# Cross-attention and routed experts on one core: the transfers of x one turn earlier, and the expert's weight address read behind the up products

## The reference, cut to what matters

```python
x = x + xattn(layernorm(x), ctx)          # 16 heads of 16, keys and values from ctx
h = layernorm(x)
probs = softmax(h @ gate_w.T)             # 8 experts
topw, sel = top_k(probs, 2); topw /= sum(topw)
g, u = split(h @ w1[e].T)                 # 176 each
out  = (silu(g) * u) @ w2[e].T            # weighted by topw, summed over the two experts
x = x + out
```

## Time and profile before

| | |
|---|---|
| median of 3 runs | 459.46 us (458.37 to 460.66) |
| profiled execution, its own time | 459.9 us |
| its span, first to last instruction | 458.2 us |
| TensorE busy | 428.8 us, 94% |
| VectorE busy | 365.5 us, 80% |
| ScalarE busy | 298.1 us, 65% |
| GpSimd busy | 278.9 us, 61% |
| share of TensorE's lines in the chain that ended last | 86% |

### The profile page before, as it was taken

One profiled execution on the slowest core, in us unless ns is written; L12 is line 12 of the kernel. 1 busy time (PEld: TensorE's weight loads), 2 busy tenths in 40 slices (PEclk: granted clock), 3 DMA queues, 4 the chain that ended last, 5 costly groups with the idle time before them and its releaser, 6 DMA issues.

```text
span 458.2 us, 15236 instructions
## 1 busy us (share of the span) xinstructions
PE 428.8 (94%) x4422; PEld 381.7 (83%) x4422; DVE 365.5 (80%) x1283; ACT 298.1 (65%) x873; POOL 278.9 (61%) x472
## 2 busy tenths in 40 slices
PE   7899899999999999999999988799999999999980
PEld 3668788988889888898898877499999999898970
DVE  7558689898898988989999786669766666888993
ACT  4465767777677777777777754456666666666650
POOL 5773447687676767767777665664445444444451
PEclk9999999999999999999999999979999999999995
DMA  7234333544423433334343333554444445789965
GB/s 215 81 110 117 105 92 109 145 143 140 143 80 98 120 93 106 98 93 122 93 119 87 97 86 109 150 173 144 136 137 130 128 142 178 228 254 333 310 215 180
DMA packets 55818, 64.62 MB, mean 141 GB/s; under 512 B 9775, under 2 KB 49210, under 8 KB 55738
## 3 DMA queue, kind: packets, MB, share of 16 engines
q1 hardware_dynamic: 45034, 42.73, 33.1%
q0 software_dynamic: 6480, 16.85, 10.5%
q10 hardware_dynamic: 4224, 4.06, 2.7%
HBM read 32.73 MB, written 23.14 MB: 122 GB/s over the span
## 4 chain that ended last, share of the span: by engine, by line
PE 86%; DVE 4%; issue 3%; DMA 3%; ACT 2%; POOL 1%; SPq 1%; POOLq 0%; DVEq 0%; ACTq 0%
PE bank L1450 14%; PE bank L1452 13%; PE bank L1451 13%; PE bank L1513 6%; PE bank L1703 4%; PE bank L1501 4%; PE bank L1460 3%; PE bank L1574 3%; PE bank L1570 3%; PE bank L1571 3%; PE bank L1572 3%; PE bank L1478 3%; PE bank L1485 2%; PE bank L1556 2%; PE bank L1737 2%
## 5 line engine op out<-in xcount | busy, mean ns | idle before, releaser
L635 POOL DMA_INDIRECT expert_out<-probs,late x71 | 70.0, 986 | 73.7 <-ACT probs L836 71.5
L558 POOL DMA_INDIRECT sorted_rows<-row,place_i x64 | 68.4, 1068 | 34.7 <-POOL row L550 24.5
L1450 PE MATMUL bank<-we_h,xt_h 128*128 x142 | 52.6, 370 | 0.6 <-DVE xt_l L1363 0.6
L728 ACT ACTIVATE probs<-bank 128x1024 f32<-128x1024 f32 x32 | 32.9, 1027 | 23.3 <-PE bank L1574 23.3
L1451 PE MATMUL bank<-we_l,xt_h 128*128 x142 | 46.4, 326 | 0.0
L1452 PE MATMUL bank<-we_h,xt_l 128*128 x142 | 46.3, 326 | 0.0
L1373 DVE SCALAR_TENSOR_TENSOR probs<-xn,late,bank 128x176 f32<-128x176 f32 x71 | 28.0, 395 | 19.9 <-ACT xn L816 19.1
L816 ACT ACTIVATE xn<-bank 128x176 f32<-128x176 f32 x71 | 22.6, 318 | 31.2 <-PE bank L1452 31.2
L1363 DVE TENSOR_TENSOR xt_l<-bank,xt_h 128x256 fp32r<-128x256 f32 x71 | 30.1, 424 | 14.2 <-ACT xt_h L810 13.3
L972 DVE TENSOR_REDUCE bank<-bank 128x16 f32<-128x1024 f32 x32 | 39.1, 1222 | 0.0
L1574 PE MATMUL bank<-neg_max_t,head_of 128*128 128x128 bf16 x256 | 35.2, 219 | 0.0
(11 more groups left out here) (233 smaller groups left out, 1563.3 us busy)
## 6 DMA issues: line engine op xcount, KB each, us to landing
late<-sorted_rows SPq DMA_DIRECT2D x71, 129.0 KB, 2.3
we_f<-w_exp SPq DMA_DIRECT2D x32, 152.0 KB, 2.3
v_bd<-v_sb SPq DMA_DIRECT2D x128, 34.0 KB, 2.3
ctx_in<-ctx_t SPq DMA_DIRECT2D x32, 128.0 KB, 2.3
qp<-q_hl SPq DMA_DIRECT2D x128, 32.0 KB
x<-x SPq DMA_DIRECT2D x13, 256.0 KB, 2.9
row<-expert_out SPq DMA_DIRECT2D x6, 512.0 KB, 4.9
qp<-expert_out SPq DMA_DIRECT2D x6, 512.0 KB, 5.3
```

The source lines that it names most:

```text
L558: pool.indirect_dma_start(sorted_rows, bass.IndirectOffsetOnAxis(ap=place_i[:, t.slot // 2, k, t.par:t.par + 1], axis=0), row[:, k, t.slot ...
L635: pool.indirect_dma_start(expert_out, bass.IndirectOffsetOnAxis(ap=hs(r)[:, D:D + 1].bitcast(U32), axis=0), y_sb[:, r % YRING, :], None, b ...
L1450: pe.matmul(dst, a_h, b_h, start=start, stop=False)
```

## The change

The transfers of `x` begin in turn 0 and end in turn 11, where they began in turn 1 and ended in turn 12. The read of the next slot's weight address moves from ahead of the transposes of slot `i` to behind the up products of slot `i-1`; what is read there in turn `i` is the address of slot `i`, which the next turn uses. The address of slot 0 is read at the start of turn 0.

```diff
@@ SyncE, the turn of the first part
-            if 1 <= j * SKEW + s <= X_THIRD + X_REST:
-                n = j * SKEW + s - 1
+            if j * SKEW + s < X_THIRD + X_REST:
+                n = j * SKEW + s
                 at = 8 + 2 * n
                 sp.dma_start(x1[:, at:at + 2, :], x_v[:, at:at + 2, :]).then_inc(x_third if n < X_THIRD else x_rest, 16)
@@ TensorE, the turn of the second part
-            if gates:
-                found[r] = weights_of(i - 1)
+            if i == 0:
+                found[1] = weights_of(0)
             if i == 1:
                 pe.wait_ge(S["x_gate_ready"], NT)
                 pe.wait_ge(S["qn_ready"], NT)
             if not static or i < NSLOT:
                 tr_hs(i, r % 2, j, r)
             if i == 1:
                 warm(kv_bank, 3)
             if gates:
                 gate_up(i - 1, (r - 1) % 2, found[r])
+            if 1 <= i < NSLOT:
+                found[(r + 1) % RING] = weights_of(i)
```

## The result

| | before | change |
|---|---|---|
| median | 459.48 us, 4 runs (458.37 to 460.66) | 454.04 us, 4 runs (453.15 to 456.11) |
| profiled execution, its own time | 459.9 us | 456.11 us |
| its span | 458.2 us | 454.4 us |

The ratio is 0.9888, with an interval of 0.9845 to 0.9930: 5.4 us less, against 6.0 forecast. The profiled execution of the change is the slowest of its four. Part of that is its start: the first transpose of x stands at 10.7 us, before at 8.9.

A forecast was written before the change was run, and what follows sets the result against it. TensorE, busy 94% of the span, was taken as the bound, so only its idle or slowed places could win time. Gains of 3.1 + 2.5 + 0.5 = 6.1 us from 459.9 gave 453.8, forecast as 453.5 us; range 451.0 to 457.2.

The forecast's parts named there:

- The transfers of x: First part, turns 5 and 13: issued one turn earlier, both VectorE waits go, 3.1 us saved; bounds 2.0 and 3.2.
- The new transfer in turn 0: Start of the first part: issued at about 10.2 us behind the setup, delays nobody; cost taken as 0, at most 0.6.
- Rival C: First part: the earlier transfers win nothing because another wait replaces the one removed; 456.5 us, chance 0.05.
- The calm stretch: Second part, slots 6 to 48: a few hundredths saved in some turns, 0.5 us taken from 0 to 2.
- The reserve of 0.35 to 0.5: Second part: sequencer's lead over the array at the moved address read, 0.35 to 0.5 us instead of 0.17.
- Rival B: Second part: the activation's transposes starve behind the moved read, 0.2 us by 67 slots; about 470 us, chance 0.06.
- The late reads: Second part, slots 48 to 70: moved address loads cover overruns better, 2.5 us saved; bounds 0 and 4.5.
- about 2.08: Second part, from slot 48 on: forecast pace in us a slot, where before had 2.204.
- Rival A: Second part: the moved read wins nothing because the sequencer is nearly full, 1.8 of 2.0 us; 456.4 us, chance 0.17.
- The start of the second part: First turns of the second part: ScalarE and VectorE set the turn, so the moved reads cost 0.
- rival D: Start of the second part: TensorE's low clock lasts over more busy turns, up to 3 us given back; 456.5, chance 0.06.

The follow-up runs named there:

- the kernel with the earlier store: The change, with ScalarE's store of results issued about 1 us earlier, behind the activation function of the same turn: 457.36 us against 460.78, ratio 0.9951.
- the thin sums: The kernel before, with VectorE's sums of finished results (lines 1413 and 1418) on 4 of 256 columns: 456.46 us in one execution, before 460.39.
- the thin stores: The kernel before, with ScalarE storing finished rows of only 16 of 128 partitions: 454.82 us in one execution, before 460.78.
- rounds 1 and 2: Variants of the change there: sums and stores one turn later, 453.68 us; sums two turns later, 453.87; read behind the activation's transposes, 455.3.
- round 3: Before with stores of 16 partitions, 454.82 us, or later stores, 459.7; the change with earlier stores, 457.36, or a second unused read, 479.5.

## Why the prediction was right, and where not

**The transfers of x (3.1 us): right.** No wait of line 947 is left, the turns take 8.3 and 8.0 us where 8.1 was forecast, 1.8 + 1.1 = 2.9. The experiment with the transfers alone gives 3.7 us in the median, somewhat more, and no run shows why. Not all of the 2.9 arrives: the first transposes of the second part come 2.0 us earlier. Over all profiles that stretch takes 278.1 to 279.1 us with the early transfers, and 282.4 once (with the second read); without them it takes 280.7 to 281.1, and 282.7 and 285.8 once each. The new transfer in turn 0 costs nothing that shows. Rival C falls.

**The calm stretch (0.5): right.** 42 by 0.009 is 0.4 us.

**The reserve of 0.35 to 0.5: right in an ordinary turn, not for long loads.** The ordinary turn shows 0.4 to 0.5, but the long loads of the kernel with the earlier store were covered by 0.2 at the median. Rival B, the activation's transposes that starve, did not happen: the list has no wait of theirs for issue in the change from 388 to 440, and behind three of its four longest loads there (0.53 to 0.65) they came 0.1 to 0.2 us late.

**The late reads (2.5 us): the step that failed.** I wrote that "the six shrink by 0.3 each, 1.8 us, and the small ones go, 0.9", with loads as long as before. Four things were otherwise. The 0.3 for each load was too large: the new place covers some 0.2 of a long load where the old one covered 0.17, so with loads as long as before (excess 6.3) the waits for issue are 2.5 us in the new place and were 2.6 in the old. The loads themselves lost 4.3 to 5.5 us of excess, which no term held, because the new place begins with ScalarE's store and not 0.9 us behind it; shown by moving the store alone, which brought the long loads back. With the long loads the issue waits went altogether, so the pace should have come near 2.02, and with one turn more for the results it did. But the fourth thing took it back: VectorE now reaches the sum before the result has landed, and the slot waits behind it, 1.7 us in one profile; in the other 2.2 and some 1.75 by the clock that falls after it. What was left of the late stretch is 1.2 us in the one and 0.1 in the other profile, against 2.5, and its pace 2.15 and 2.20, where about 2.08 was named as the sign. I had bounded the term by how long loads are and how far they are covered, and had not asked the prediction's own question there, what is late next. The row that answers it was in reach, in the trace of before: the first ten transfers of results land 3.9 to 6.3 us after their issue there, while the sums are placed by a count of turns. The one issued at 410.6 landed 4.6 us later, and its sum began at 415.89, only 0.7 us behind. (The results come back from slot 45 on, the first is issued at 385.3, and not from about slot 51 as said above.)

**Rival A, that the read wins nothing,** is not excluded by the medians: the read is worth about 1 us, less than half of 3.0, and the interval of the read alone reaches none. Its reason is. The sequencer's count of 1.8 us was near the 1.7 found, but it did not bind; the results' transfer did.

**The sum.** 3.1 + 2.5 + 0.5 was forecast as the gain. In the medians it is 3.7 for the transfers and 1.3 for the read, 5.0, or 5.4 by the first comparison. That the total is so near is luck in part: the first part gave more than its term, and in the second a cover put too large and a wait put at nothing met loads that became shorter for a reason nobody had forecast. The start of the second part was costed at 0. The table shows 1.35 us less there in the change, but this goes with the clock: the lower level lasts 6.8 us before and in the transfers alone (6.9), where that stretch takes 16.4 us, 3.4 us in the change and in most others (15.0 to 15.6), and is absent in the thin sums (14.1). Kernels with the order of before stand in all three groups. So it varies with the execution. No loss of the kind of rival D shows at that place.

**Open** is why a register load grows behind a store. With fewer bytes, of loads or of stores, the loads were shorter, in one execution each. It is not the store's own bytes that a load meets, at least not always. The load of 1.31 us in before was over at 403.86, and from 402.5 to 403.9 the view of the DMA queues has only these two:

```profile
q1 hardware_dynamic: 75, 0.31, 70.9%
q0 software_dynamic: 1, 0.00, 0.7%
```

The stores are in queue 10 (its bytes fall from 4.06 to 0.62 MB with the thin stores), so the store issued at 401.65 had not moved a byte yet. The load of 1.18 us with the earlier store is the same case: no packet of queue 10 from 393.2 to 394.5. What such a load does meet no row tells, nor why a distance of 1.9 to 2.6 us can be long again. Open too is whether the later sums are worth having: they save 4.0 us up to slot 70 and give back 1.6 behind it in one pair of profiles, and the medians do not decide.

## What to carry to other kernels

When a wait shrinks in a pipeline that is paced by one engine, look at everything that is placed by a count of turns and waits for a transfer: faster turns bring its consumer forward, not its data. Give it the turn that was won, and check what that adds behind the last turn. And an instruction whose duration varies with traffic is placed by its distance from the transfers that are issued near it, not only by what covers it.

## What the runs showed of the hardware

- A register load on TensorE's sequencer takes 0.30 us as a rule. While results are stored and loaded back it took over 0.4 and up to 1.55 in 45 of the 50 cases in which it began about 0.9 us behind the issue of a whole 256 KB store, and at most 0.32 in the 59 cases of the change and its variants of rounds 1 and 2 in which it began within 0.25 us of it, before or behind. In round 3 two of 16 that began within 0.3 us of the issue, before or behind it, were long (0.57 and 0.83), so the place is a good one and no guarantee. The Trainium skill, page "DMA: Bandwidth & Descriptors", section "Latency and other measured facts", has a floor of about 600 ns for such a load; no trace here agrees, the median is 304 ns.
- In one execution of the change TensorE's clock fell to the lower level behind a single pause: the up products came 2.2 us late, and then it ran 3.5 us at 0.51. The DMA engines had a share of 0.95 before the fall and 0.96 in it. In the other profile of the change, three pauses of up to 0.9 us did not bring it down.
- An unused read of some 0.65 us on TensorE's sequencer cost 0.35 us in each slot of the calm stretch, and the execution took 479.5 us, 25 more than the change's median.
